# Moving the ranks of a counting sort into the gather pass before it, and looking up two quads a slot in the placing stage

## The reference, cut to what matters

```python
x = _layernorm(x + _L0_gnn_ref(x, edge_index))                 # gather x[dst], sum by src
x = _layernorm(x + _L1_gnn_ref(x, L1_gnn_W, edge_index, ...))  # (x @ W[rel])[src], sum by dst
x = _layernorm(x + _L2_gnn_ref(x, src, dst, edge_weight1, ...))# edge MLP, sum by src, node MLP
x = _layernorm(x + _L3_gnn_ref(x, edge_index, ...))            # two graph convolutions, sum by dst
```

## Time and profile before

| | us |
|---|---|
| median of 3 runs | 6499.26 (6485.71 to 6501.09) |
| span of the profiled execution | 6462.1 |
| first gather pass `e0`, first put of POOL to the last group | 955 to 1640 |
| placing stage `place_and_relate` | about 1646 to 2343 |
| POOL's scatters in it | 1670.5 to 2324 |

### The profile page before, as it was taken

How to read it: one execution, slowest core, us unless ns; L and a number is a source line. 1 busy time by engine, 2 the same in 40 slices (tenths; PEclk the granted TensorE clock), 3 DMA queues, 4 the chain that set the end, 5 groups by cost and what they waited for, 6 DMA issues and landing times. The chain is left out here.

```text
span 6462.1 us, 74448 instructions
## 1 busy us (share of the span) xinstructions
PE 3919.6 (61%) x19983; PEld 3086.7 (48%) x19983; DVE 2177.2 (34%) x4653; ACT 1422.3 (22%) x3080; POOL 2886.1 (45%) x2799
## 2 busy tenths in 40 slices
PE   3333451668656742667466759888952669626697
PEld 2122121667422322666265646776732668426586
DVE  7444790324645620124311102343530112102134
ACT  0000000001333420112200126443420223302135
POOL 2555406663566766661555540000146660366602
PEclk8555575555666765555555569999975555755569
DMA  3000131111445641223734436554631222412235
GB/s 99 2 2 2 47 113 33 43 42 42 155 175 202 234 153 38 66 70 138 264 99 101 107 116 202 181 180 181 227 113 35 69 69 84 145 36 69 69 106 177
DMA packets 354959, 692.13 MB, mean 107 GB/s; under 512 B 183337, under 2 KB 185254, under 8 KB 339130
## 3 DMA queue, kind: packets, MB, share of 16 engines
q1 hardware_dynamic: 148381, 491.73, 21.7%
q10 hardware_dynamic: 118428, 130.12, 6.0%
q0 software_dynamic: 87808, 66.01, 5.8%
HBM read 350.87 MB, written 349.58 MB: 108 GB/s over the span
## 5 line engine op out<-in xcount | busy, mean ns | idle before, releaser
L1058 PE MATMUL e_ring<-e_msgs,e_hot 128*128 x6272 | 1419.4, 413 | 1091.3 <-issue 1082.7
L1058 PEld LDWEIGHTS e_ring<-e_msgs,e_hot 128*128 128x128 f32 x6272 | 1385.0, 328 | 1127.4 <-issue 1125.9
L925 POOL DMA_INDIRECT e_msgs<-y,index_D x784 | 741.4, 946 | 640.9 <-POOLq L77 261.1
L977 DVE TENSOR_TENSOR e_hot<-e_nodes,keys_D 128x2048 f32<-128x2048 f32 x147 | 336.9, 2292 | 1596.9 <-remote 872.0
L599 POOL DMA_INDIRECT list_D<-d_place,d_target x392 | 456.2, 1164 | 326.6 <-DVEq L553 210.5
L925 POOL DMA_INDIRECT e_msgs<-y,index_S x392 | 396.8, 1012 | 387.7 <-DVE index_S L963 198.3
L599 POOL DMA_INDIRECT list_S<-s_place,s_target x392 | 390.6, 996 | 362.8 <-DVEq L553 247.5
L1241 POOL DMA_INDIRECT m_far<-x,index_S x392 | 390.9, 997 | 347.9 <-DMA pairs_by_edge<-m_far 221.4
L1410 PE MATMUL m_ring<-m_region,m_hot 128*128 x1568 | 375.9, 426 | 215.7 <-issue 213.3
L925 POOL DMA_INDIRECT e_msgs<-x_by_relation,index_D x392 | 374.0, 954 | 210.4 <-issue 112.8
L1410 PEld LDWEIGHTS m_ring<-m_region,m_hot 128*128 128x128 f32 x1568 | 348.1, 328 | 244.3 <-issue 242.2
(11 more groups left out here) (368 smaller groups left out, 5846.1 us busy)
## 6 DMA issues: line engine op xcount, KB each, us to landing
x_by_relation<-d_stage SPq DMA_DIRECT2D x98, 1024.0 KB
agg<-e_stage ACTq DMA_DIRECT2D x196, 256.0 KB
n_in<-agg SPq DMA_DIRECT2D x42, 896.0 KB, 5.6
x<-n_out SPq DMA_DIRECT2D x28, 896.0 KB, 3.6
m_keyrow<-keys_by_step SPq DMA_DIRECT2D x49, 512.0 KB
m_region<-pairs_by_edge SPq DMA_DIRECT2D x49, 512.0 KB
messages<-m_region SPq DMA_DIRECT2D x98, 256.0 KB
m_region<-messages SPq DMA_DIRECT2D x49, 512.0 KB, 4.1
```

The costliest lines, as they stand in the source:

```text
L925: pool.indirect_dma_start(out=msgs[:, (i % HELD) * D:(i % HELD + 1) * D], out_offset=None, in_=source, in_offset=bass.IndirectOffsetOnAxis ...
L977: nc.vector.tensor_tensor(hot[g % 2][:, :, :], bc(nodes[:, 0:P].unsqueeze(1), [P, GS, P]), bc(order["keys"][:, g * GS:(g + 1) * GS].unsque ...
L1058: mm = nc.tensor.matmul(ring[:, bass.ds(bucket, D)], hot[g % 2][:, k, :], msgs[:, bass.ds(tile, D)], start=False, stop=False, skip_group_c ...
```

## The change

The ranks of the D order need only the low digits of the keys, which exist from the second group of `e0` on. The change makes the ranks of 84 of the 98 quads inside `e0`: after each of the groups 3 to 31 and 36 to 48 PE spreads the keys of two quads into two PSUM banks that the histogram had used, and DVE ranks them after the go of the next group. The result is kept in a new buffer `rank_dst`; an index buffer that nothing reads (`index_S2`) goes away. In the placing stage the remaining 14 quads are ranked in slots 0 to 13, and each slot transposes, copies and looks up two quads (`LOOKED = 2`), so that the lookups take slots 0 to 48 and unit u's targets are made in slot 7(u+1)//2: 3, 7, 10, 14 and so on to 49. Norm, products and stores stay in their slots.

```diff
+RANKED_AGAIN = 36
+RANKED = tuple(range(3, 32)) + tuple(range(RANKED_AGAIN, GROUPS))
+EARLY_RANKS = 2 * len(RANKED)
+LOOKED = 2
...
-    def dve_rank(self, dve, q):
-        h = q % 2
-        of = self.p_k[q % len(self.p_k)]
-        dve.wait_ge(self.sem("spread"), q + 1)
-        if q >= 2:
-            dve.wait_ge(self.sem("rank"), q - 1)
+    def dve_rank(self, dve, q, begin=0):
+        i = q - begin
+        h = i % 2
+        of = self.p_k[i % len(self.p_k)]
+        dve.wait_ge(self.sem("spread"), i + 1)
+        if i >= 2:
+            dve.wait_ge(self.sem("rank"), i - 1)
...
-    def dve_unit(self, dve, u):
+    def dve_unit(self, dve, u, begin=0):
...
-        dve.wait_ge(self.sem("rank"), UQ * (u + 1))
+        if UQ * (u + 1) > begin:
+            dve.wait_ge(self.sem("rank"), UQ * (u + 1) - begin)
...
     def pe_spread(self, pe, q):
+        self.pe_keys(pe, q)
+        self.pe_hots(pe, q)
+
+    def pe_keys(self, pe, q, begin=0):
         n = len(self.p_k)
-        if q >= n:
-            pe.wait_ge(self.sem("rank"), q - n + 1)
+        i = q - begin
+        if i >= n:
+            pe.wait_ge(self.sem("rank"), i - n + 1)
...
+    def pe_hots(self, pe, q):
         if q >= len(self.p_ht):
             pe.wait_ge(self.sem("hott"), q - len(self.p_ht) + 1)
...
 # stair_pass
+            sort.ranking(sb, [spare[1 + h][:, :].rearrange("p (j e) -> p j e", e=P) for h in range(2)],
+                         K["rank_dst"])
+            ranked = {g: (2 * i, 2 * i + 1) for i, g in enumerate(RANKED)}
...
 # DVE, in the loop over the groups
                     if g == 35:
                         sort.dve_table(dve)
+                    for q in ranked.get(g - 1, ()):
+                        sort.dve_rank(dve, q)
...
 # PE, in the loop over the groups
                     if g == 33:
+                        pe.wait_ge(sort.sem("rank"), 2 * sum(r < 33 for r in RANKED))
                         sort.pe_steps(pe)
+                    if g == RANKED[0]:
+                        pe.wait_ge(s_keyt, 2)
+                    if g == RANKED_AGAIN:
+                        pe.wait_ge(sort.sem("steps"), 1)
+                    for q in ranked.get(g, ()):
+                        sort.pe_keys(pe, q)
...
 # place_and_relate
+        unit_at = {UQ * (u + 1) // LOOKED: u for u in range(CHUNKS)}
+        hots_at = {UQ * u // LOOKED - 2: u for u in range(1, CHUNKS)}
...
 # DVE
-                    s = (c - 2) * UQ + n
-                    if c < CHUNKS:
-                        sort.dve_rank(dve, c * UQ + n)
-                    if n == 0 and 1 <= c <= CHUNKS:
-                        sort.dve_unit(dve, c - 1)
-                    if n == 2 and c + 1 < CHUNKS:
-                        hots(c + 1)
+                    at = c * UQ + n
+                    s = at - 2 * UQ
+                    if at in unit_at:
+                        sort.dve_unit(dve, unit_at[at], EARLY_RANKS)
+                    if EARLY_RANKS + at < QUADS:
+                        sort.dve_rank(dve, EARLY_RANKS + at, EARLY_RANKS)
+                    if at in hots_at:
+                        hots(hots_at[at])
...
 # PE
-                    if c < CHUNKS:
-                        if n == 0:
-                            pe.wait_ge(sort.sem("onehot"), c + 1)
-                        sort.pe_spread(pe, q)
-                    if 1 <= q <= QUADS:
-                        sort.pe_lookup(pe, q - 1)
+                    for q in range(LOOKED * at, LOOKED * (at + 1)):
+                        if q < QUADS:
+                            if q % UQ == 0:
+                                pe.wait_ge(sort.sem("onehot"), q // UQ + 1)
+                            sort.pe_hots(pe, q)
+                        if 1 <= q <= QUADS:
+                            sort.pe_lookup(pe, q - 1)
+                    if EARLY_RANKS + at < QUADS:
+                        sort.pe_keys(pe, EARLY_RANKS + at, EARLY_RANKS)
...
 # ACT
-                    if c < CHUNKS:
-                        sort.act_hott(act, c * UQ + n)
+                    for q in range(LOOKED * at, LOOKED * (at + 1)):
+                        if q < QUADS:
+                            sort.act_hott(act, q)
```

More of the change, by code:

```diff
@@ L294, in histogram, with ranking, placing @@
         self.steps_i = sb("steps_i", [1, STEPS])
-    def placing(self, sb, tile_high, unit_low, p_k, p_ht, p_v):
+    def ranking(self, sb, p_k, held=None):
+        self.p_k = p_k
+        if held is None:
+            self.rank = sb("rank", [P, T])
+        else:
+            self.rank = held[:, :]
+        self.scratch = sb("scratch", [P, 2, QUAD, P], BF16)
+    def placing(self, sb, tile_high, unit_low, p_ht, p_v):
         self.tile_high, self.unit_low = tile_high, unit_low
-        self.p_k, self.p_ht, self.p_v = p_k, p_ht, p_v
+        self.p_ht, self.p_v = p_ht, p_v
         self.place = sb("place", [P, T, 4], I32)
         self.target = sb("target", [P, T], I32)
-        self.rank = sb("rank", [P, T])
         self.hott = [sb(f"hott{h}", [BH, QUAD, P], BF16) for h in range(2)]
-        self.scratch = sb("scratch", [P, 2, QUAD, P], BF16)
         self.found = sb("found", [P, UNIT, 2, BL])
@@ L636, in order_sources @@
                        p_v, [p[:, :, :].rearrange("p a b -> p (a b)") for p in p_k], p_deg[0])
-        sort.placing(sb, lambda t: hot_h[:, t, :], lambda u: hot_l[:, u * UNIT:(u + 1) * UNIT, :], p_k, p_ht, p_v)
+        sort.ranking(sb, p_k)
+        sort.placing(sb, lambda t: hot_h[:, t, :], lambda u: hot_l[:, u * UNIT:(u + 1) * UNIT, :], p_ht, p_v)
         degree = sb("degree", [P, T])
@@ L1017, in _ @@
                         sort.dve_table(dve)
+                    for q in ranked.get(g - 1, ()):
+                        sort.dve_rank(dve, q)
+            if sort is not None:
+                for q in ranked.get(GROUPS - 1, ()):
+                    sort.dve_rank(dve, q)
         @block.tensor
@@ L1576, in place_and_relate @@
         sort.digits(sb)
+        sort.ranking(sb, p_k, K["rank_dst"])
         sort.placing(sb, lambda t: part_h[t // UNIT % 2][:, t % UNIT, :], lambda u: part_l[u % 2][:, :, :],
-                     p_k, p_ht, p_v)
+                     p_ht, p_v)
+        unit_at = {UQ * (u + 1) // LOOKED: u for u in range(CHUNKS)}
+        hots_at = {UQ * u // LOOKED - 2: u for u in range(1, CHUNKS)}
         s_in = [sem(f"in{h}") for h in range(2)]
@@ L1749, in _ @@
                 for n in range(UQ):
-                    q = c * UQ + n
-                    s = (c - 2) * UQ + n
-                    if c < CHUNKS:
-                        if n == 0:
-                            pe.wait_ge(sort.sem("onehot"), c + 1)
-                        sort.pe_spread(pe, q)
-                    if 1 <= q <= QUADS:
-                        sort.pe_lookup(pe, q - 1)
+                    at = c * UQ + n
+                    s = at - 2 * UQ
+                    for q in range(LOOKED * at, LOOKED * (at + 1)):
[7 more added lines that the diff above has]
+                        sort.pe_keys(pe, EARLY_RANKS + at, EARLY_RANKS)
                     if s >= 0:
@@ L2337, in gnn @@
                       "table": sb(f"table_{n}", [1, STEPS], I32), "gates": sb(f"gates_{n}", [1, GROUPS, 2], U16), "banks": sb(f"banks_{n}", [1, 64], U16)}
-                  for n, columns in (("S", (0, 2)), ("D", (0, 2)))}
+                  for n, columns in (("S", (0,)), ("D", (0, 2)))}
         orders["S"]["halves"] = sb("halves", [1, 2 * GROUPS, 2], U16)
@@ L2385, in gnn @@
         prior16 = sorted_by("prior16", [BH, T, 2, BL], BF16)
+        K["rank_dst"] = sorted_by("rank_dst", [P, T])
         for order in orders.values():
```

2 lines of the change are left out of this document (1 added, 1 removed).

## The result

The changed kernel takes 6642.03 us (median of 4 runs, 6633.79 to 6661.61), the kernel before 6500.18 (4 runs, 6485.71 to 6529.88): ratio 1.0211, 95% interval 1.0186 to 1.0236. It is 142 us slower; 129 were predicted.

The account below looks back on a forecast made before the run. No engine full in placing: its end set by POOL's 392 scatters, with slots slow beside them, and fast slots without POOL. Placing +84 and e0 +45 make +129 us; on 6499.3 that gives 6628, rounded 6625; range 6420 to 6740.

Parts of the forecast that it names:

- The mechanism: Placing and gather: PE and hand-offs slow severalfold 20 to 25 us into unbroken POOL runs; about 3 us pause clears it.
- The block of 28: Placing stage: POOL's 28 scatters take 38.4 us, against 40.9 before, with half the DVE collisions saved; 538 us in all.
- The pauses: Placing stage: POOL runs dry five times for some 6 us, 30 us in all, bounds 0 and 80.
- What is left: Placing after POOL's end at 2230: 50 of 112 slots, 67 MB at 340 GB/s, 197 us; stage +84 us.
- e0: Early ranks in this gather pass: PE gains 1.08 us a group over 42 groups, +45 us; bounds 14 and 150.
- The tail's term: Last 13 groups of e0, PE 99.8% busy: added key spreads surely on the path, 14 us.
- The bound of 150: Upper bound in e0: each hand-off of spread keys seen late, up to 3.5 us more a group.
- The first: Rival, placing: slots don't suffer beside POOL once ranks are gone; about -108 us with e0, 6390; chance 0.18.
- The second: Rival, placing: lighter slots from 49 on run ahead, 75 to 85 done by POOL's end; 6480 to 6545; chance 0.20.
- The third: Rival, e0: stalls on late spreads, +150 us there, placing as forecast; 6735; chance 0.12.
- The fourth: Rival, placing: two lookups take as long as two slots, POOL starves as now; +200 us, 6740; chance 0.05.

Follow-up runs that it names:

- y2: The changed kernel with POOL held to one unit of puts per seven slots, slow chip: 6443.46 us against 6441.85 for the kernel before, ratio 1.0009.
- v1: The kernel before, POOL waiting ahead of every four puts for a lookup, in source-ordering and placing stages, slow chip: 6314.85 us against 6452.89, ratio 0.9787.
- y1: The changed kernel itself, run again on another slow chip: 6581.39 us against 6441.85 for the kernel before, ratio 1.0204.
- x1: The changed kernel with one lookup a slot in place of two, fast chip: 5192.18 us against 5176.73 for the kernel before, ratio 1.0023.
- z1: The kernel before with SP also moving 252 half chunks in the source-ordering stage, fast chip: 5182.75 us against 5179.83, ratio 1.0008.
- x2: The changed kernel with POOL held to one unit of puts per seven slots, fast chip: 5169.26 us against 5176.73 for the kernel before, ratio 0.9977.
- x4: The changed kernel without early ranks, two ranks and two lookups a slot, fast chip: 5176.84 us against 5176.73 for the kernel before, ratio 1.0002.
- z4: The changed kernel without early ranks and with POOL held to one unit per seven slots, fast chip: 5240.51 us against 5179.83 before, ratio 1.0121.

## Why the prediction was right, point by point

*The mechanism.* "Some 20 to 25 us after POOL begins an unbroken run of indirect DMAs, PE and its hand-offs slow down by a factor of several, and a pause of about 3 us clears it." The first half holds on the chip of the result and on the three others of its kind, and not as a rule: the onset in the source-ordering stage is about 10 us, y2's slots ran beside 280 puts, and on the two fast chips it is absent. The second half holds for runs of 28 puts and v1's shorter ones, and not for the long runs that the change brings: there the late signals took up to 14.6 us to arrive. That the change loses by letting POOL run ahead is shown by y1 and y2, which differ in one wait: 803 against 638 us of placing. The second lookup's round trip and the early ranks are in both. The lateness explains ACT's and DVE's waits, not all of PE's: in e0 PE itself stands idle for 0.9 to 2.5 us between single matmuls without a wait that the profile shows (`<-issue`), and why is open.

*POOL.* The block of 28 was put at 38.4 us; 392 puts in 620 us less 79 of pauses are 38.7. Its reason holds as well: in the kernel before, 109 puts overlap a DVE TENSOR_TENSOR of 0.9 us or more and 40 of them take over 2 us, while none of the other 283 takes over 0.98; in the changed kernel 53 overlap, about half, and 19 of them take over 2 us. The pauses were the mis-sized term: five of 6 us, 30 in all, against four, 79 in all; three of the four are 20 to 26 us (y1: 53 in all). The prediction took the slots to be fast as soon as POOL stops. In the first pause the late signals arrive 7.5 to 14.6 us after POOL's last put, and only then do the slots go on to the next unit's targets: two copies pass in the 26 us ahead of 2007. The 79 us are the upper bound of 80 that the prediction had kept for its range.

*What is left.* 62 of 112 slots were to be done at POOL's end; 46 copies and the 14 slots that have none are 60. The tail was to be 197 us at 340 GB/s; from POOL's end at 2333.9 to the stage's end at 2520.3 it is 186, and 176 of them run at 395 GB/s. The stage's busiest stretch before had 329 GB/s beside loads, and the allowance for having none was too small. In all the stage was to take 16 + 538 + 30 + 197 = 781 us and takes 17.1 + 541.2 + 78.9 + 186.4 = 823.6: the miss of +42 (+126 for +84) is the pauses, +49, less the tail, -11, and 4 of small change. In y1 the stage is 803 us long, 106 more than in the profile of before. The sum in microseconds is nearer than its parts: on the two profiles the two stages come to +164 where +129 was said, and the medians, 142 us apart, hide that, as the first profile is of a short execution and the second of a long one. That much of the closeness is luck. y1 gives +135 by its stages and +140 by its median.

*e0.* +45 was said, +37.5 measured (+29 in y1). The tail's term was 1.08 us a group and is 7.68 - 6.84 = 0.84: each group's matmuls follow at once on eight spreads that take 0.85, so four take 0.43 where 0.54 was taken. In the crawling part POOL resumes at 1202.7, 1242.7, 1283.3 and 1323.1, every three groups; the period of 35.5 us (the earlier trace rows has one such put, the next came at 1269.52) has become 40.1, 1.5 us a group and more than 1.08; the 29 groups of it would make 44 us, but the ends of the groups in the two traces show the growth in the first 18 of them only: against the entry of e0 the changed kernel is 27 us behind at group 20 and still 27 at group 35, and the last 13 groups add 10. In between, the kernel before has longer waits of its own (63 us from group 31 to group 34, against 56). The bound of 150 (late spreads) didn't come. On the fast chip e0 takes 533 to 539 us with the ranks and without: there they are free.

*The rivals.* The first, slots that don't suffer, is the picture of the fast chips: the slots keep up and the stage ends 11 us after POOL's last put. The Trainium skill's page "SBUF — State Buffer", section "Who interferes with whom", says of the ports of the SBUF that PE and ACT never wait on anyone. Taken as a rule for their hand-offs, which is more than it says, no cast would be late; x1 agrees (56 of 56 within 0.05 us), and the kernel before on a slow chip doesn't (up to 16.4 us). But even there the gain of 108 us that the prediction gave this rival would not come: POOL already streams without a wait in the kernel before (z1, whose placing stage is that of the kernel before, makes its 392 puts in one run and takes 607 us), so looking up faster has nothing to shorten. The changed kernel itself was not run on such a chip; x1, x2 and x4, each a part of it or all of it with a wait, are within 0.3%. The second, lighter slots that run ahead, wanted 75 to 85 slots done at POOL's end, and 60 were. The third is the bound of 150 above. The fourth, "no faster feeding", is refuted by the runs of 196 and 56 puts.

*Open.* What holds PE's work or its signal back in the chip isn't shown, nor how the chips differ. Nor is it settled why y2 got through 280 puts. One reading, argued from rows and not tested: while slots run, DVE's 2 us operations hold POOL back now and then, which may act as pauses. In y2, 26 of the 127 puts from 2000 to 2200 take over 2 us; in the crawl of the changed kernel, 1790 to 1980, 3 of 145. y2's timelines of DVE and POOL:

```profile
2082.34 2.02 DVE L1708 TENSOR_TENSOR d_value<-d_got_a,dis 128x1792 f32<-128x1792 f32 x1
...
2082.97 2.23 POOL L618 DMA_INDIRECT list_D<-d_place,d_target  x1 [0.30 <-issue]
2085.49 2.77 POOL L618 DMA_INDIRECT list_D<-d_place,d_target  x1 [0.30 <-issue]
2088.57 0.97 POOL L618 DMA_INDIRECT list_D<-d_place,d_target  x1 [0.30 <-issue]
```

It would make the crawl feed itself, as both the run of 196 and that of 280 suggest: stopped slots leave POOL's stream unbroken. Another is the prediction's second rival: y2's last lookup copy of ACT is at 1970.2, so all the slots from 2000 on are the light ones, while every slow slot of the changed kernel beside POOL had lookups in its time. Against it, y2's last four slots have no lookups either and crawl. Also, y2 should by its stages (+30 in e0, -60 in placing, against the profile of before on another chip) be some 30 us faster than before and is level; its profiled span is 15 us under its median, and the rest is within the interval.

## What to carry to other kernels

An engine that is fed earlier doesn't only finish earlier: look at what its longer unbroken run does to the others, here by dating what one engine finished and when the next one starts on it. If signals are late while one engine streams, try waits that tie the stream to the others' progress, so that it pauses briefly and often instead of long and seldom; one such wait gave 2.1% on a slow chip (v1) where moving 84 ranks and doubling the lookups cost 2.1%. And run both versions on more than one kind of chip before calling either tuned. A wait that holds POOL to the slots took 165 us off one kernel's stage on a slow chip (y1, y2), did nothing for it on a fast one (x2) and cost another kernel 1.2% there (z4); v1 was run on a slow chip alone.

## What the runs showed of the hardware

- The same program takes 5177 and 5180 us on two chips and 6442, 6453, 6500 and 6528 on others. The mean granted clock of TensorE is 0.67 to 0.68 on the former and 0.63 to 0.64 on the latter, but e0 is 533 to 539 us against 696 to 699 with the same granted clock of 0.51 in it (x1, the kernel before), and the last put of the source-ordering stage starts 524 to 553 us after the first, against 659 to 672 (traffic and added waits apart).
- On the slow kind, ACT starts on PE's finished work up to 24 us late beside a stream of indirect DMAs from POOL in the source-ordering stage, and catches up within 5 us of POOL's stop behind runs of 28 puts. In the placing stage of the changed kernel, behind a run of 196 puts, it takes 14.6 us. DMA traffic of 340 GB/s beside it is not needed for it and doesn't cure it.
- An indirect DMA of POOL takes 0.97 us to issue by itself and up to 2.8 us when it overlaps a DVE TENSOR_TENSOR (40 of 109 over 2 us in the kernel before); beside a TENSOR_REDUCE alone 43 of 43 take 0.97.
